# Cross attention of 64 batches: sums taken inside the product of the values, product turned and divided by token

## The reference

```python
q = (x @ Wq).reshape(B, N, HEADS, hd).transpose(0, 2, 1, 3)
k = (context @ Wk).reshape(B, M, HEADS, hd).transpose(0, 2, 1, 3)
v = (context @ Wv).reshape(B, M, HEADS, hd).transpose(0, 2, 1, 3)
scores = jnp.einsum('bhid,bhjd->bhij', q, k) * scale      # hd = 8
attn = jax.nn.softmax(scores, axis=-1)                    # over 77 tokens
out = jnp.einsum('bhij,bhjd->bhid', attn, v)
out = out.transpose(0, 2, 1, 3).reshape(B, N, DIM)
return out @ Wo
x = _layernorm(x + _L0_xattn_ref(x, ...), axis=-1)
```

## Time and profile before

| | |
|---|---|
| timed runs | 1484.57, 1484.61, 1485.5 us |
| profiled execution, first to last instruction | 1482.30 us (the profile gives no other time of its own) |
| PE busy | 1369.5 us, 92% |
| DVE busy | 1197.3 us, 81% |
| ACT busy | 873.4 us, 59% |
| POOL busy | 1167.6 us, 79% |
| mean granted clock of PE | 0.976 |
| cross attention | from about 163 to 555 us |

### The profile page before, as it was taken

One profiled execution on the slowest core, in us unless ns is written; L12 is line 12 of the kernel. 1 busy time (PEld: TensorE's weight loads), 2 busy tenths in 40 slices (PEclk: granted clock), 3 DMA queues, 4 the chain that ended last, 5 costly groups with the idle time before them and its releaser, 6 DMA issues. The chain is left out here.

```text
span 1482.3 us, 34966 instructions
## 1 busy us (share of the span) xinstructions
PE 1369.5 (92%) x12862; PEld 1092.1 (74%) x12862; DVE 1197.3 (81%) x2379; ACT 873.4 (59%) x1542; POOL 1167.6 (79%) x1036
## 2 busy tenths in 40 slices
PE   4765699999999977999999999996999999999998
PEld 3554566666666655777777777765999999999997
DVE  5998467766776766888888888886999999999996
ACT  2777444544544534777777777764566666666665
POOL 6344466666666645999999999995999999999997
PEclk8999599999999998999999999999999999999999
DMA  5110343333333305222222222212233233232231
GB/s 157 38 35 27 94 123 94 99 103 105 98 94 94 92 20 171 79 79 79 79 79 78 79 79 78 79 71 69 69 93 88 79 92 87 79 93 86 80 93 29
DMA packets 77195, 123.81 MB, mean 84 GB/s; under 512 B 8354, under 2 KB 45795, under 8 KB 77027
## 3 DMA queue, kind: packets, MB, share of 16 engines
q1 hardware_dynamic: 75426, 117.16, 25.2%
q0 software_dynamic: 1088, 4.19, 1.0%
q10 hardware_dynamic: 512, 0.23, 0.1%
HBM read 70.28 MB, written 51.27 MB: 82 GB/s over the span
## 5 line engine op out<-in xcount | busy, mean ns | idle before, releaser
L971 POOL TENSOR_TENSOR gather_d<-gather_e,gather_rinv 128x1024 f32<-128x1024 f32 x128 | 244.9, 1913 | 44.6 <-DVE gather_rinv L950 44.6
L1230 POOL TENSOR_TENSOR mix_c<-mix_e,mix_rinv 128x1024 f32<-128x1024 f32 x128 | 240.9, 1903 | 17.4 <-DVE mix_rinv L1218 13.4
L1298 PEld LDWEIGHTS last_Y<-kept_phi,last_cT 128*128 128x128 f32 x2048 | 248.3, 192 | 7.1
L1298 PE MATMUL last_Y<-kept_phi,last_cT 128*128 128x128 f32 x2048 | 249.1, 275 | 0.0
L1314 ACT COPY last_cT<-last_T 128x1024 f32<-128x1024 f32 x128 | 128.4, 1003 | 128.8 <-PE last_T L1305 128.8
L1215 DVE TENSOR_REDUCE mix_sums<-mix_e 128x16 f32<-128x1024 f32 x128 | 155.9, 1218 | 32.8 <-ACT mix_e L1189 32.6
L946 DVE TENSOR_REDUCE gather_rsum<-gather_e 128x32 f32<-128x1024 f32 x128 | 156.1, 1220 | 26.2 <-ACT gather_e L919 26.2
L797 POOL TENSOR_TENSOR cross_kd<-first_pack,kept_consts 128x624 fp32r<-128x624 f32 x128 | 155.5, 1236 | 18.9 <-DMA first_pack<-first_halves 12.5
L965 POOL TENSOR_TENSOR gather_dl<-gather_d,gather_dh 128x512 fp32r<-128x512 f32 x128 | 166.2, 1299 | 0.0
L641 ACT ACTIVATE cross_pT<-cross_P 77x1024 f32<-77x1024 f32 x128 | 130.3, 1021 | 49.7 <-PE cross_P L568 49.7
L908 ACT COPY gather_keep<-gather_L 128x256 f32<-128x256 f32 x256 | 94.7, 370 | 104.2 <-PE gather_L L882 97.2
(11 more groups left out here) (195 smaller groups left out, 3166.2 us busy)
## 6 DMA issues: line engine op xcount, KB each, us to landing
kept_logits<-gather_keep SPq DMA_DIRECT2D x128, 256.0 KB, 2.0
mix_read<-kept_logits SPq DMA_DIRECT2D x64, 512.0 KB, 3.7
first_halves<-first_qk SPq DMA_DIRECT2D x32, 412.0 KB, 3.7
first_pack<-first_halves SPq DMA_DIRECT2D x64, 128.0 KB
first_pack<-first_halves SPq DMA_DIRECT2D x32, 206.0 KB
first_pack<-first_halves SPq DMA_DIRECT2D x64, 78.0 KB
attn_xTg<-in_xT SPq DMA_DIRECT2D x16, 256.0 KB, 2.8
kept_xres<-in_x POOLq DMA_DIRECT2D x4, 1024.0 KB, 12.8
```

The lines of the kernel that those rows point to most:

```text
L971: pool.tensor_tensor(dd[u % 4][:].rearrange("p i (n s) -> p i n s", n=16), e[u % 2][:], rinv[u % 2][:].rearrange("p (i n) -> p i n", i=2). ...
L1230: pool.tensor_tensor(self.cc[u % 2][:], self.e[u % 2][:], self.rinv[u % 2][:].unsqueeze(2).to_broadcast([128, 16, EXPERTS]), ALU.mult)\
L1298: ins = pe.matmul(psY[t % 2][:, 0:128], cT[u % 2][:, c, :], w.yk[:, 8 * (u % 2) + c, :], start=(u % 2 == 0 and c == 0), stop=(u % 2 == 1 a ...
```

## The change

The sums are no longer a product of their own. Each head gets 16 columns: its 8 values, a column of ones, and 7 of zeros. Two heads share one product of 32 columns, so that eight heads fill the 128 partitions of `psO[:, 0, :]` and the other eight those of `psO[:, 1, :]`. ACT copies both to SBUF (`oS`), PE turns them (`turn_products`) into `psO[:, 2:4, :]`, token-major, where each head's sum is one column. DVE takes the reciprocal of 128 x 16 sums and divides with a broadcast of them over 8 features. PE turns the result back (`turn_context`) and ACT copies it to `oT`. The rows of Wo stay in an order of two halves (`by_half`).

Besides, the projections of queries, keys and values stand ahead of the scores; `turn_x2` of n-4 becomes that of n-5, stands ahead of the turned scores and writes to the first quarter of the first bank of `psP` instead of `psM` (but for the last five batches); the statistics (`aggregate`) move to the start of the next step, and with them `normalise` on POOL; there is one step more.

```diff
-        vd = [st.sb(f"vd{i}", [128, 8, 160]) for i in range(3)]
-        od = st.sb("od", [128, 160])
+        vd = [st.sb(f"vd{i}", [128, 8, 96]) for i in range(3)]
-        rs = st.sb("rs", [128, 128])
+        oS = st.sb("oS", [128, 2, 128])
+        rs = st.sb("rs", [128, 16])
+        on = [st.sb(f"on{i}", [128, 128]) for i in range(2)]
-        psO = st.ps("O", [128, 2, 128])
+        psO = st.ps("O", [128, 4, 128])
+        by_head = psO[:, 2:4, :].rearrange("t g (x k) -> t (g x) k", k=16)
-        STEPS = range(-1, B + 4)
+        STEPS = range(-1, B + 5)
+        SHARED = B - 5
+        def x2_turned(n):
+            return banks[:, 0, 0, :] if n < SHARED else psM[:, 0:128]
...
             def turn_x2(n):
                 pe.wait_ge(x2_kept, n + 1)
-                take_bank(xl_ready, n + 1)
-                pe.transpose(psM[:, 0:128], w.xres[:, tokens(n)], w.ident).then_inc(xT_made, 1)
+                if n < SHARED:
+                    pe.wait_ge(e_low, n + 5)
+                else:
+                    take_bank(xl_ready, n + 1)
+                pe.transpose(x2_turned(n), w.xres[:, tokens(n)], w.ident).then_inc(xT_made, 1)
             def turned_scores(n):
                 reach(pe, e_ready, n)
+                reach(pe, xl_ready, n - 4)
...
+            def values(n):
+                pe.wait_ge(vd_ready, n // 2 + 1)
+                pe.wait_ge(e_ready, n + 1)
+                reach(pe, oT_ready, n)
+                for g in range(2):
+                    for i in range(2):
+                        for q in range(4):
+                            ins = pe.matmul(psO[32 * q:32 * q + 32, g, :],
+                                            vd[n // 2 % 3][:, 4 * (n % 2) + q, 48 * g + 16 * i:48 * g + 16 * i + 32],
+                                            pT[n % 2][:, 2 * g + i, q, :], start=(i == 0), stop=(i == 1),
+                                            skip_group_check=True)
+                ins.then_inc(av_made, 1)
+
+            def turn_products(n):
+                pe.wait_ge(oS_ready, n + 1)
+                for g in range(2):
+                    ins = pe.transpose(psO[:, 2 + g, :], oS[:, g, :], w.ident)
+                ins.then_inc(o_turned, 1)
+
+            def turn_context(n):
+                pe.wait_ge(on_ready, n + 1)
+                pe.transpose(psO[:, 0, :], on[n % 2][:], w.ident).then_inc(on_turned, 1)
...
             for n in STEPS:
-                if is_batch(n):
-                    scores(n, 0)
                 for r in projected(n):
                     queries_keys(r)
                 for r in valued(n):
                     own_values(r)
+                if is_batch(n):
+                    scores(n, 0)
                 if is_batch(n - 2):
-                    values(n - 2, 0)
+                    values(n - 2)
                 if is_batch(n):
                     scores(n, 1)
-                if is_batch(n - 2):
-                    values(n - 2, 1)
                 if is_batch(n - 3):
                     project(n - 3)
+                if is_batch(n - 5):
+                    turn_x2(n - 5)
                 if is_batch(n - 2):
-                    sums(n - 2, 0)
+                    turn_products(n - 2)
                 if is_batch(n):
                     turn_max(n)
                     turned_scores(n)
-                if is_batch(n - 4):
-                    turn_x2(n - 4)
-                if is_batch(n - 2):
-                    sums(n - 2, 1)
...
                     shift(n)
+                if is_batch(n - 2):
+                    turn_context(n - 2)
...
         # ACT, behind the exponentials of n - 1
+                if is_batch(n - 2):
+                    act.wait_ge(av_made, n - 1)
+                    reach(act, o_turned, n - 2)
+                    act.copy(oS[:], psO[:, 0:2, :]).then_inc(oS_ready, 1)
+                if is_batch(n - 5):
+                    act.wait_ge(xT_made, n - 4)
+                    act.copy(w.xh[0:127, tokens(n - 5)], x2_turned(n - 5)[0:127]).then_inc(xh_ready, 1)
                 if is_batch(n):
                     ...
                     act.copy(mT[:], psM[:, 0:128]).then_inc(mT_ready, 1)
+                if is_batch(n - 2):
+                    act.wait_ge(on_turned, n - 1)
+                    reach(act, pj_made, n - 3)
+                    act.copy(oT[n % 2][:], psO[:, 0, :]).then_inc(oT_ready, 1)
...
             def invert_sums(n):
-                dve.wait_ge(av_made, n + 1)
-                reach(dve, oT_ready, n)
-                dve.reciprocal(rs[:], psO[:, 1, :]).then_inc(rs_ready, 1)
+                dve.wait_ge(o_turned, n + 1)
+                reach(dve, on_ready, n)
+                dve.reciprocal(rs[:], by_head[:, :, 8]).then_inc(rs_ready, 1)
             def divide(n):
                 dve.wait_ge(rs_ready, n + 1)
-                reach(dve, pj_made, n - 1)
-                dve.tensor_tensor(oT[n % 2][:], psO[:, 0, :], rs[:], ALU.mult).then_inc(oT_ready, 1)
+                reach(dve, on_turned, n - 1)
+                dve.tensor_tensor(on[n % 2][:].rearrange("t (x e) -> t x e", e=8), by_head[:, :, 0:8],
+                                  rs[:].unsqueeze(2).to_broadcast([128, 16, 8]), ALU.mult).then_inc(on_ready, 1)
...
         # DVE, in step n
+                if is_batch(n - 4):
+                    aggregate(n - 4)
                 if is_batch(n):
                     peak(n, 0)
...
                 if is_batch(n - 3):
                     add_residual(n - 3)
-                    aggregate(n - 3)
-                if is_batch(n - 4):
-                    low_part(n - 4)
+                if is_batch(n - 5):
+                    low_part(n - 5)
```

More of the change, by code:

```diff
@@ L458, in attend_context @@
         kd_ready, v_made, vd_ready = (st.sem(n) for n in ("kd_ready", "v_made", "vd_ready"))
-        s_made, mx_ready, m_made, mT_ready, e_ready, av_made, rs_ready, oT_ready = (
-            st.sem(n) for n in ("s_made", "mx_ready", "m_made", "mT_ready", "e_ready", "av_made", "rs_ready",
-                                "oT_ready"))
+        s_made, mx_ready, m_made, mT_ready, e_low, e_ready, av_made, oS_ready, o_turned, rs_ready, on_ready, on_turned, \
+            oT_ready = (
+                st.sem(n) for n in ("s_made", "mx_ready", "m_made", "mT_ready", "e_low", "e_ready", "av_made", "oS_ready",
+                                    "o_turned", "rs_ready", "on_ready", "on_turned", "oT_ready"))
         pj_made, y_done, st_done, mv_ready, ve_done, rstd_ready, x2_kept, xT_made, xh_ready, xl_ready = (
@@ L640, in exponentials @@
                 hs = slice(2 * half, 2 * half + 2)
-                ins = act.activation(pT[n % 2][0:J, hs, :, :], psP[:, hs, :, :], ACT.Exp)
-                if half == 1:
-                    ins.then_inc(e_ready, 1)
+                act.activation(pT[n % 2][0:J, hs, :, :], psP[:, hs, :, :], ACT.Exp)\
+                    .then_inc(e_ready if half == 1 else e_low, 1)
             def weights_high(c):
@@ L668, in _ @@
                     reach(act, av_made, 2 * r - 4)
-                    act.copy(blocks(vd[r % 3][0:J]), psM[0:J, 0:256].rearrange("j (c h e) -> j c h e", c=8, h=4))\
-                        .then_inc(vd_ready, 1)
+                    act.copy(heads(vd[r % 3][0:J])[:, :, :, 0:8],
+                             psM[0:J, 0:256].rearrange("j (x i e) -> j x i e", i=2, e=8)).then_inc(vd_ready, 1)
                 if is_batch(n - 1):
                     exponentials(n - 1, 1)
+                if is_batch(n - 2):
[5 more added lines that the diff above has]
+                    act.copy(w.xh[0:127, tokens(n - 5)], x2_turned(n - 5)[0:127]).then_inc(xh_ready, 1)
                 if is_batch(n):
@@ L676, in _ @@
                     act.copy(mT[:], psM[:, 0:128]).then_inc(mT_ready, 1)
-                if is_batch(n - 4):
-                    act.wait_ge(xT_made, n - 3)
-                    act.copy(w.xh[0:127, tokens(n - 4)], psM[0:127, 0:128]).then_inc(xh_ready, 1)
+                if is_batch(n - 2):
+                    act.wait_ge(on_turned, n - 1)
+                    reach(act, pj_made, n - 3)
+                    act.copy(oT[n % 2][:], psO[:, 0, :]).then_inc(oT_ready, 1)
         @block.vector
@@ L689, in clear_values @@
             def clear_values(i):
-                dve.memset(vd[i][:], 0.0).then_inc(vd_clear, 1)
+                dve.memset(vd[i][:], 0.0).then_inc(vd_zero, 1)
+                dve.wait_ge(vd_zero, i + 1)
+                dve.memset(heads(vd[i][:])[:, :, :, 8], 1.0).then_inc(vd_clear, 1)
             def split_low(r):
@@ L1451 @@
     by_dim = np.arange(D).reshape(4, 32).T.reshape(D)
+    by_half = np.arange(D).reshape(4, 2, 16).transpose(1, 0, 2).reshape(D)
     host = {
```

26 lines of the change are left out of this document (8 added, 18 removed).

## The result

The changed kernel takes 1435.51 us in the median of four runs (1433.06 to 1437.55), the kernel before 1485.05 beside it: a ratio of 0.9667, with a 95% interval of 0.9654 to 0.9679. It is 3.3% faster, 49.5 us. The profiled execution spans 1434.0 us, 48.3 less than before.

What follows compares the result with a forecast made beforehand. A loop over PE and DVE was taken to bound the 5.88 us step. 60 steps x (5.88 - 5.45) = 25.8 us, less 1.9 for the longer drain, gave 1461 us; forecast's own range 1452 to 1470, 8-in-10 range 1449 to 1478.

Steps and rivals of the forecast that it cites:

- The old bound: Context attention stage: a loop over PE (3.76 us) and DVE (2.12 us) through the reciprocal sets the 5.88 us step.
- Costs of the new operations: Changed stage, on ACT and DVE: product's copy 0.37 us, turned context's copy 0.27, reciprocal 0.27, division 0.29.
- The new loop: Chain from scores through reductions, residual, low part, turned scores, shift, turn and projection: 5.62 even, 5.27 odd, mean 5.45 us.
- the turned context's slot: PE, between shift and the next step: turning the context back takes 0.26 us, a term of the loop.
- The drain: End of the stage, last shift to next stage's first matmul: one extra step costs 0 to 3.8 us, taken as 1.9.
- PE's own list: PE's slots in one step summed: 5.55 us even, 5.20 odd, just below the loop.
- rival C: Attention steps: the loop is shorter than read, only PE's slots count; step 5.2 us, 1446 us; chance 0.13.
- a credit of 0.23: PE's projection slots: lower estimate takes 0.23 us off, 0.93 to 0.70 even, 0.57 to 0.34 odd.
- Rival B: Hand-overs to ACT and back outlast their cover; step 5.60 to 5.85 us, 1470 to 1485 us; chance 0.16.
- the cover of the turned context: DVE's reciprocal and division take 0.68 us while PE needs 1.04 for turned scores and shift: 0.36 us to spare.
- The other cover: Road over ACT to turn_products: 3.31 us against 3.82 until PE gets there, slack stated as 0.4.
- Rival D: PE is granted the lower clock, 1.2 GHz, in part of the stage; with every second step 1521 us; chance 0.09.

Runs made afterwards that it cites:

- b_small_recip: The kernel before with the reciprocal taken of 16 columns instead of 128, the others left undivided: 1469.32 us, ratio 0.9899.
- a_ctx_mid: The changed kernel with turn_context one place earlier, between the turned scores and shift, in steps that have both: 1447.78 us, ratio 0.9748.
- a_ctx_twice: The changed kernel with turn_context issued twice into the same place: 1447.04 us, ratio 0.973.
- a_first_split: The changed kernel with first scores ahead of the projections and values in two parts with the second scores between them: 1425.54 us, ratio 0.9592.
- b_both_joined: The kernel before with a quarter of the products with ones, the reciprocal of 16 columns, and values in one piece ahead of second scores: 1492.02 us, ratio 1.0044.
- a_x2_own_turn: The changed kernel with turn_x2 of all batches in the shared bank, between output projection and turned maxima: 1546.18 us, ratio 1.0418.
- a_stats_early: The changed kernel with the statistics moved back right behind the residual, ahead of the low part: 1453.5 us, ratio 0.9786.

## Why the prediction was wrong, point by point

**The old bound: right.** The loop over reciprocal, division and reduction was the bound, and PE's list lay 0.2 us below it; b_small_recip shows both.

**Costs of the new operations: right**, all within 0.02 us.

**The new loop: nearly the right chain, three of four terms too large.** This is the step of the sum that failed, and the turned context's slot, 0.26 us predicted and 0.01 found, is its largest part. By the starts in the timeline after (even step from 399.64 to 404.75, odd step from 394.80 to 399.64):

| term | predicted | measured |
|---|---|---|
| first scores to second scores | 1.51 | 1.55, 1.52 |
| second scores to turned scores | 2.13 | 1.97, 1.97 |
| turned scores, shift | 0.92 | 0.85, 0.85 |
| turned context and projection, even | 1.06 | 0.74 |
| the same, odd | 0.71 | 0.50 |
| step | 5.62, 5.27 | 5.11, 4.84 |

The turned context's slot of 0.26 us I had copied from turn_x2, a transpose that stood between products of another tile. At the end of the step it lies beside full-size work, and adds next to nothing (the next weights start 0.01 us behind its own); in a_ctx_mid the slot is 0.25 us again and the step 0.17 to 0.21 us longer, and in the trace of a_ctx_twice one transpose more costs 0.11. The second error: I added DVE's durations end to end, and they overlap: residual and low part start 0.73 and 0.93 us behind the start of a reduction of 0.81. By that the chain to the low part is no longer last, if only by some 0.05 us (the low part ends at 403.73, the turned scores start at 403.90, and my hop was 0.12); the turned scores stand behind the turned maxima, and these wait for the residual.

60 x (5.45 - 5.00) is 27 us, the whole miss; with the 2.7 us of the stall, which no term of mine had, the equal steps were even shorter. The drain was right: from the last shift to the next stage it is 16.93 us (487.55 to 504.48) where it was 15.34, so the extra step cost 1.6 us against 1.9; the 0.2 of the table above is that less a last step shortened by 1.4. 1.5 us more at the start and 2.9 behind the stage, which I had taken as unchanged, offset a part of the miss. Nothing behind the stage is changed in any kernel here, and in the fourteen profiles it takes 926.6 to 931.7 us; batch 3 starts at 179.9 to 184.3 us. So neither difference can be told from that spread.

**PE's own list: over-counted, and so rival C was priced too high.** I had it at 5.55 and 5.20 us. In a_first_split the same products and one more change of tile pass in 4.95 and 4.72. The list I wrote down summed slots read in a kernel in which each contained a change of tile; in the even step above the output projection, turn_x2 and the turning of the product follow one another at 0.22 and 0.17 us (starts 402.42, 402.64 and 402.81), for which I had 0.5 and 0.26. C's sum has an error besides: it speaks of a credit of 0.23 twice and takes off 0.2. With 0.46 it gives 4.92 us and 1429 us, and the equal steps are 4.98. C's sign, no wait at the turned scores, was seen. Its mechanism, PE as the only bound, did not hold to the end: PE has a hole of 0.3 to 0.4 us ahead of the turned maxima.

**Edits that I had called cheap.** The move of the statistics I never named as a gain: my chain ran from the residual straight to the low part, so the sum has it, and it carries 18 us; the bank of turn_x2 I treated as a slot, and without it the kernel is slower than before. Both belong to the chain on DVE behind the second scores, the bank to its part up to the turned maxima, the statistics to its part up to the low part. That they were in the profile's reach is plain: 0.5 us of DVE work stood ahead of the low part and the reciprocal.

**Rival B** (hand-overs eat the gain): refuted in the main; the cover of the turned context was 0.4 to 0.5 us, as the 0.22 us per step for 0.70 us of added reciprocal show. The other cover was overrated. Its own terms, 3.82 and 3.31, give 0.5 and not 0.4, and yet in odd steps PE does wait for ACT's copy ahead of turn_products: 0.14 us (397.70 to 397.84). The hole ahead of the turned maxima is smaller there, 0.29 instead of 0.42 us, so the loop does not grow by it.

**Rival D** (the clock): it did not happen to the change but for one short stretch behind the stall (0.91 from 200 to 220 us; from 220 to 500 us it was 1.00), but it is real: b_both_joined, with PE idle for 0.97 us at one place in each step, and a_x2_own_turn, with 0.75 to 0.97 us at one place and 0.56 at a second, had mean clocks of 0.85 to 0.93 in the stage and lost some 30 to 40 us by the clock alone, by the estimates above. Both have no more transposes per step than the kernel they are made from. The Trainium skill, TensorE: Matmul & The Clock Gate, Part 4, holds that work in transpose mode does not count as busy for the gate in the same way. The change has four transposes per step, a_ctx_twice five, and in both the clock was 1.00 from 220 us to the end of the steps, so the rule, as far as this kernel can show it, made no difference.

## What to carry to other kernels

Where two bounds lie close together, price a change by what both lose: here a loop over DVE and PE's own list were 0.2 us apart, one saving alone gave 7 us, the other 15, both together 32. A slot read from start to start belongs to its neighbours as much as to the instruction; before moving it into a sum, look what tile stands on either side in the new place. And the order of small operations on the engine that closes a loop can weigh as much as the products removed.

## What the runs showed of the hardware

A single 128x128 transpose on PE took 0.25 us from start to start between products of 32-row tiles, and a second one put behind it next to full-size work made the step 0.11 us longer. DVE started an operation up to 0.08 us ahead of the end of the one before (402.52 + 0.81 against 403.25), where no wait stood between. And a PE that waits in every step can be granted the lower clock again and again, though it never stands still for more than 1 us: so it was in b_both_joined and a_x2_own_turn, and not in a_stats_early, where the clock was 1.00 from 200 to 480 us. What sets them apart is open. The busy shares do not settle it: b_both_joined shows 84.45 of 100 us and a_stats_early 84.56, but the former includes work at the lower clock, which takes longer, and at full clock its steps are 0.82 to 0.84 busy. Nor does the number of holes, for a_x2_own_turn has two.
